# A mixture-of-experts layer on eight cores: a fourth w1 buffer, w2 loads in quarters, and the routing transposes moved

## What is computed

```python
x = _layernorm(x + attention(x))      # local window of 256 keys plus 64 pooled latents, 16 heads, gated
x = _layernorm(x + ffn(x))

# ffn: 8 experts of 1024 -> 4096 -> 1024, two chosen for each token
router_logits = x @ router_w.T + router_b + 0.1 * expert_weights
router_probs = softmax(router_logits)
top_p, top_i = jax.lax.top_k(router_probs, 2)
top_p = top_p / top_p.sum(axis=-1, keepdims=True)
h = gelu(jnp.einsum('bsd,edh->bseh', x, w1) + b1)
expert_out = jnp.einsum('bseh,ehd->bsed', h, w2) + b2
return (top_p[..., None] * jnp.take_along_axis(expert_out, top_i[..., None], axis=2)).sum(axis=2)
```

## Time and profile before

| | us |
|---|---|
| median of 2 runs | 5319.88 (5317.14 to 5322.62) |
| the profiled execution | 5318.32 |
| its span on the slowest core, core 2 | 5316.8 |
| spans of the 8 cores | 5295.5 to 5316.8 |
| PE busy | 4527.2 (85%) |
| DVE busy | 973.5 (18%) |
| ACT busy | 902.9 (17%) |
| POOL busy | 326.1 (6%) |
| DMA | 346.66 MB, mean 65 GB/s |

### The profile page before, as it was taken

The page is one execution under the profiler, slowest core; times in us unless marked ns, Lnnn a source line. Parts: engine busy times, 40 slices in busy tenths (PEclk is TensorE's granted clock), DMA queues, the critical chain, the costliest instruction groups (busy, mean ns, idle before and its releaser), DMA issues.

```text
span 5316.8 us, 72833 instructions; the slowest of 8 cores (5295.5 to 5316.8 us)
## 1 busy us (share of the span) xinstructions
PE 4527.2 (85%) x29399; PEld 2996.8 (56%) x29608; DVE 973.5 (18%) x3181; ACT 902.9 (17%) x1493; POOL 326.1 (6%) x622
## 2 busy tenths in 40 slices
PE   8865565555469999999999999999999999999993
PEld 8533333333227475665747566584756758476671
DVE  1344555544401010000101000010100001010004
ACT  0011111111120302112030211203021120302112
POOL 1000000000000101000010100101010010100000
PEclk5866665566589999999999999999999999999996
DMA  6120000000163433444343443434344343444431
GB/s 156 43 53 20 20 21 11 21 21 21 49 144 68 78 72 62 84 71 76 68 79 70 67 81 70 78 66 80 74 70 78 66 82 62 80 79 65 82 56 64
DMA packets 121848, 346.66 MB, mean 65 GB/s; under 512 B 32874, under 2 KB 33002, under 8 KB 112370
## 3 DMA queue, kind: packets, MB, share of 16 engines
q0 software_dynamic: 86768, 281.11, 30.5%
q1 hardware_dynamic: 34754, 60.87, 3.5%
HBM read 601.97 MB, written 20.97 MB: 117 GB/s over the span
## 4 chain that ended last, share of the span: by engine, by line
PE 79%; DVE 9%; DMA 4%; issue 4%; ACT 1%; another core or an unknown queue 1%; DVEq 1%; ACTq 0%; SPq 0%; POOL 0%; POOLq 0%
PE pb L1049 34%; PE pb L1023 32%; DMA w1b<-w 3%; PE pb L577 2%; PE pb L256 2%; PE pb L750 2%; PE pb L477 1%; DVE Pt L654 1%; PE pb L844 1%; PE pb L316 1%; DVE comb L589 1%; PE pb L634 1%; PE pb L736 1%; DMA x_in<-x_comb 1%
## 5 line engine op out<-in xcount | busy, mean ns | idle before, releaser
L1023 PE MATMUL pb<-x1T_sb,w1b 128*128 128x512 bf16 x8016 | 1793.4, 384 | 167.2 <-DMA w1b<-w 85.0
L1049 PE MATMUL pb<-w2b,hT 128*128 128x256 bf16 x16384 | 1791.1, 273 | 16.9 <-ACT hT L1031 16.9
L1049 PEld LDWEIGHTS pb<-w2b,hT 128*128 128x128 bf16 x16384 | 1602.0, 98 | 209.5 <-issue 24.3
L1023 PEld LDWEIGHTS pb<-x1T_sb,w1b 128*128 128x128 bf16 x8192 | 807.6, 99 | 1149.6 <-issue 210.4
L1031 ACT ACTIVATE hT<-pb,b1all 128x512 bf16<-128x512 f32 x1024 | 703.2, 687 | 2876.8 <-PE pb L1023 2874.7
L1059 DVE SCALAR_TENSOR_TENSOR acc<-pb,c_sb,acc 128x256 f32<-128x256 f32 x512 | 247.7, 484 | 3521.1 <-PE pb L1049 3521.1
L94 POOL DMA_DIRECT2D w1b<-w x512 | 270.2, 528 | 2859.8 <-PE pb L1023 1655.6
L647 ACT ACTIVATE Pt<-pb 128x384 bf16<-128x384 f32 x256 | 122.0, 490 | 445.3 <-PE pb L634 441.6
L677 PE MATMUL pb<-Vroll,Pt 128*128 128x65 bf16 x768 | 84.1, 235 | 79.7 <-DVE Pt L654 43.5
L634 PE MATMUL pb<-QT,Kroll 128*128 128x128 bf16 x768 | 117.6, 298 | 31.3 <-PE pb L677 9.8
L94 POOL DMA_DIRECT2D w2b<-w x64 | 33.8, 528 | 1740.3 <-PE pb L1049 1620.1
(11 more groups left out here) (132 smaller groups left out, 1458.2 us busy)
## 6 DMA issues: line engine op xcount, KB each, us to landing
w1b<-w POOLq DMA_DIRECT2D x512, 256.0 KB, 3.7
w2b<-w POOLq DMA_DIRECT2D x64, 2048.0 KB, 13.7
x_in<-x_comb SPq DMA_DIRECT2D x34, 512.0 KB, 3.5
x_tc<-x_comb SPq DMA_DIRECT2D x16, 512.0 KB, 4.0
x1s<-x_tc SPq DMA_DIRECT2D x16, 512.0 KB, 2.6
acc<-x1s SPq DMA_DIRECT2D x1, 8192.0 KB, 73.5
out<-acc SPq DMA_DIRECT2D x16, 512.0 KB, 2.6
x1Ts<-x1T_tc SPq DMA_DIRECT2D x16, 256.0 KB, 2.7
```

The costliest lines, as they stand in the source:

```text
L1023: e.matmul(PB[bk][:, :], w1b[sl][:, kc * 128:(kc + 1) * 128], x1T_sb[:, kc * 2048 + Tt * 1024 + nh * 512: kc * 2048 + Tt * 1024 + (nh + 1) ...
L1049: e.matmul(PB[ob][:, 0:256], hT[:, f * 1024 + tcl * 128: f * 1024 + tcl * 128 + 128], w2b[sl2][:, f * 256:(f + 1) * 256], start=(f == 0), ...
```

## The change

It has four parts.

- **w1 buffers.** Four instead of three; at the start of stage 3 four blocks are loaded, and each block's end triggers the load of the block four further on. Room for the buffer (2 KB on each partition) comes in part from `id_b`, which goes together with its load, and from a narrower `stat`.
- **w2 loads.** Each load of a quarter is issued as four DMAs of a fourth of its columns (128 x 2048), one behind the other; only the first waits. The consumer waits for all four.
- **Routing transposes.** The transpose (L906) and the copy (L910) go from the end of each chunk. In their place, 16 transposes in four rounds, with one copy of 8 x 512 for each round, stand between stage 2 and the first matmul of stage 3, in PSUM banks 6 and 7. Each round waits for the copy of the round before it.
- **The gate.** `FGATE` now ends with `CC` of the last chunk in place of its `CTEV`.

```diff
-        id_b = sb("id_b", [128, 128], BF16)
-        stat = sb("stat", [128, 64], F32)
+        stat = sb("stat", [128, 48], F32)
-        p.new_sem("gs_idb")
-        IDB = p.dma("g", id_b[:, :], ident_in, "gs_idb")
+        IDB = None
...
-                    p.op("t", lambda e, tc=tc:
-                         e.transpose(PB[5][0:8, 288:416], c_sb[:, tc * 8:(tc + 1) * 8], id_f[:, :]),
-                         deps=[CC, rtr_rd[1 - rslot]])
-                    CTMM = p.mark("t")
-                    CTEV = p.op("v", lambda e, tc=tc:
-                                e.tensor_copy(cT[0:8, tc * 128:(tc + 1) * 128], PB[5][0:8, 288:416]),
-                                deps=[CTMM], mark=True)
-                    rtr_rd[rslot] = CTEV
+                    cc_toks.append(CC)
+                    rtr_rd[rslot] = CC
...
-                w1b = [sbf1(f"w1b{i}", [128, 1024], BF16) for i in range(3)]
+                w1b = [sbf1(f"w1b{i}", [128, 1024], BF16) for i in range(4)]
...
-                    sl = idx % 3
+                    sl = idx % 4
                     tok = p.dma("g", w1b[sl][:, :], w1_in[e_, f, :, :], f"w1sem{sl}",
-                                deps=[w1_war[sl]] + (FGATE if idx < 3 else []))
+                                deps=[w1_war[sl]] + (FGATE if idx < 4 else []))
...
-                    tok = p.dma("g", w2b[sl][:, :], w2_in[e_, dq, :, :], f"w2sem{sl}",
-                                deps=[w2_war[sl]] + (FGATE if idx < 2 else []))
+                    tok = None
+                    for c4 in range(4):
+                        tok = p.dma("g", w2b[sl][:, c4 * 2048:(c4 + 1) * 2048],
+                                    w2_in[e_, dq, :, c4 * 2048:(c4 + 1) * 2048], f"w2sem{sl}",
+                                    deps=([w2_war[sl]] if c4 == 0 else []) +
+                                         (FGATE if idx < 2 and c4 == 0 else []))
...
+                load_w1(3)
                 load_w2(0)
                 load_w2(1)
+
+                ct_ev = None
+                for rnd in range(4):
+                    cb = 6 + rnd % 2
+                    for j in range(4):
+                        tcg = rnd * 4 + j
+                        p.op("t", lambda e, tcg=tcg, j=j, cb=cb:
+                             e.transpose(PB[cb][0:8, j * 128:(j + 1) * 128],
+                                         c_sb[:, tcg * 8:(tcg + 1) * 8], id_f[:, :]),
+                             deps=[cc_toks[tcg], EPB[6] if cb == 6 else EPB[7], ct_ev])
+                    tkc = p.mark("t")
+                    ct_ev = p.op("v", lambda e, rnd=rnd, cb=cb:
+                                 e.tensor_copy(cT[0:8, rnd * 512:(rnd + 1) * 512],
+                                               PB[cb][0:8, 0:512]),
+                                 deps=[tkc], mark=True)
+                CT_LAST = ct_ev
...
-                            if iw1 + 3 < len(seq_w1):
-                                load_w1(iw1 + 3)
+                            if iw1 + 4 < len(seq_w1):
+                                load_w1(iw1 + 4)
```

More of the change, by code:

```diff
@@ L434, in build_program @@
                 CC = None
+                cc_toks = []
                 LEXP = None
@@ L945, in build_program @@
                 CCLAST = CC
-                CT_LAST = rtr_rd[1]
                 EPB5X = pb5_ex
@@ L973, in build_program @@
                             b1_in.rearrange("e p f -> p e f"), "b1sem", deps=FGATE)
-                for i in range(3):
+                for i in range(4):
                     p.new_sem(f"w1sem{i}")
@@ L977, in build_program @@
                     p.new_sem(f"w2sem{i}")
-                w1_war = [None, None, None]
+                w1_war = [None, None, None, None]
                 w2_war = [None, None]
```

## The result

Part of the executions, of both kernels and of some in the experiments, ran with the clock of one die held lower, for which my range of 5200 to 5256 us had no room (with them the medians are 5455.79 us for the changed kernel, 12 runs, and 5815.41 us for the one before, 10 runs), so all times compared below, also those of the experiments, are of the others. These took 5225.01 to 5253.70 us with the change and 5316.03 to 5322.62 us before; their ratio is 0.984, with a 95% interval of 0.9809 to 0.9871. The profiled execution of the changed kernel took 5230.22 us, against 5318.32 before: 88.1 us less. My 5220 lies 10 us under it. What follows is about the 88 us.

The account below looks back on a forecast made before the run. PE bounds the kernel in the expert lines, standing at each phase handover for a w1 block queued behind w2. 5318.3 - 61 (buffer) - 25 (clock) + 0 (quarters) - 14.4 (transposes) + 1.3 (stage 3 start) gave 5220 us, range 5200 to 5256.

Parts of the forecast that it names:

- The fourth buffer: Phase handovers of the experts: one more w1 block in place shortens PE's waits for w1, 61 us less.
- its landing stays: Phase handovers: the fifth w1 block, still behind w2, lands when the fourth did, so each wait shrinks by 3.45 us.
- the expected hit of POOL's late issue: Experts: POOL's late w2 issue meets one handover instead of four; such waits were 6.42 to 6.52 us, not about 3.8.
- The clock: Experts: with shorter waits PE's matmuls mostly keep the full clock; 25 us less, 6 of 31 us staying.
- The assumption between the rows: Phase handovers: waits of 2.5 us and less keep the full clock; the trace has none between 1.04 and 3.76.
- The quarters: POOL's queue: w2 loads in four pieces move the same bytes one behind the other, so 0 us change.
- The transposes: Stage 2: without the transpose DVE starts the next chunk sooner, 0.9 us for each of 16 chunks, 14.4 us less.
- 0, if another wait was as late: Stage 2: low end of the saving from moving the routing transposes, no gain if another wait ends as late.
- The start of stage 3: Start of stage 3: `x1T_sb` lands some 15 us earlier, but the wait for ACT grows by as much; +1.3 us.
- the low clock: Rival, experts: waits near 2 us still lower the clock and some hits stay, 5250 us; chance 0.14.
- the pieces in series: Rival, POOL's queue: each added w2 piece pays 2.4 us ahead of the w1 blocks, 5363 us; chance 0.04.
- the full gain: Rival, phase handovers: all waits go as quarters land sooner in the early phases too, 5197 us; chance 0.16.

Follow-up runs that it names:

- e2: The kernel before with the fourth w1 buffer alone (w2 loads whole, transposes in their old place): 5233.11 us.
- e6: The changed kernel with each phase's last w2 load issued in four pieces behind the w1 loads of blocks 2, 4, 6 and 8 of the next phase: 5203.68 us.
- e4: The changed kernel with the small load of `b1all` ahead of `x1T_sb` and `acc` on SP's queue: 5221.6 us.
- e3: The kernel before with the w2 loads in quarters alone, three w1 buffers: 5311.89 us.
- e1: The kernel before with the routing transposes moved behind stage 2 and the new gate alone: 5324.7 us, beside 5320.1 before.
- e8: The changed kernel with two added DVE operations that nothing needs after `c_sb` of each chunk: 5229.86 us.
- e9: The changed kernel without the eight multiplications by the latent mask, which leaves the causal mask of the latent attention out: 5216.85 us.
- e5: The changed kernel with six added DVE operations that nothing needs after `c_sb` of each chunk: 5266.81 us.

## Why the prediction was right or wrong

**The fourth buffer, -61 us: right.** The w1 waits of the slowest core fell by 65.8, and the mean of the cores agrees (88.7 us off phases 2 to 16, with the clock). That core 7's first waits (5.24, 2.91, 1.50, 2.31) come near the 5.0, 3.4, 2.5, 2.3 that I worked out for core 2 is luck: core 2 itself now waits 0.33, 0.31, 1.28 and 0.36 us there, and core 7 had 3.85, 3.74, 3.98 and 3.70 before. The long early waits fall on one core of a pair, and not on the same one each time; my list put them down to core 2. The list of waits also adds up to nearly 23 us with its hit, where I wrote 21. One step inside it failed: "its landing stays". In phase 15 of core 2 it did (14.03 us after, 14.06 before), but on core 7 the block lands 15.45 us into phase 16 (4912.22 less 4896.77), where 14.3 was usual on that core. e2, whose w2 loads are whole, has it too (15.2 us in phases 7, 8 and 10), so the pieces are not why. It may be the other core's traffic; that was not tried. PE stood 0.8 to 1.5 us there in six of the phases 6 to 16, and the expected hit of POOL's late issue did not come on core 7, which made up for it.

**The clock, -25 us: right within 5 us.** The experts shrank by 85.8, of which 65.8 are waits, so 20 us of the 31 at half clock came back. e6 gives the floor, 3357 us without a wait: core 7 lies 29 us over it, of which 19.2 are w1 waits, so 10 us or a little less are left where I had left 6. The assumption between the rows was half right: 2.44 us (e2) kept the full clock, 2.31 us (phase 5 after) lowered it, 1.50 did not. A stretch after the wait of 1.50 us (phase 4) and one after that of 2.31 (the columns as in the windows above):

```profile
2211.50:2216.00 4.50, 4.43 (x21) 2.08 (x22) 0.00 (x0) 1.37 (x2) 0.28 (x1) 1.00 0.75 139
...
2438.00:2444.00 6.00, 6.00 (x21) 2.38 (x20) 0.00 (x0) 1.38 (x2) 0.32 (x1) 0.72 0.36 68
```

So it is not the length of the wait alone that decides: 2.31 us lowered the clock and 2.44 did not. In e4 a wait of 2.43 us on core 4 lowered it too, with 98.54 us for the same 448 matmuls that take 96.85 at the full clock:

```profile
2190.21 98.54 PE L1036 MATMUL pb<-x1T_sb,w1b 128*128 128x512 bf16 x448 [2.43 <-DMA w1b<-w]
```

**The quarters, 0: right in size**, at +0.1 us from issue to landing in phase 15 of e3, and a gain by the way that I had put under the buffer: 48 DMAs a phase move POOL's late issue off the handover.

**The transposes, -14 us: wrong, and this is the step that failed.** "The chain of DVE sets the end", I wrote, so that 0.9 us go for each chunk. They went, at the place that I named. But further down the chain stand 16 matmuls that run at either clock, and I priced them as fixed, though the profile's row of granted clock (0.5 to 0.6 through this stage) said that they are not. Two of 14 us remained on the mean of the cores (1068.7 to 1066.8), and 0.9 at the gate, which now follows the last `c_sb` by 0.5 us in place of 1.4; e1 shows it in isolation and e8 in reverse. I had named "0, if another wait was as late" as an end of this term, but looked for a wait and not for a clock. The profile's row before, 40 slices of 133 us in tenths of full speed, of which stage 2 takes the fifth to the eleventh:

```profile
PEclk5866665566589999999999999999999999999996
```

**The start of stage 3, +1.3 us: right**, at +2.4. `x1T_sb` lands 27.6 us after the gate, 19 sooner than before (I said some 15), and it bought nothing, for the reason given. The quarters alone (e3) bring it to 26 to 29 us over the cores. The rows that answer to the earlier trace rows:

```profile
1465.23 9.20 PE L1036 MATMUL pb<-x1T_sb,w1b 128*128 128x512 bf16 x32 [22.28 <-DMA x1T_sb<-x1Ts]
1517.64 2.72 PE L1036 MATMUL pb<-x1T_sb,w1b 128*128 128x512 bf16 x6 [43.21 <-ACT hT L1044]
...
1515.52 1.28 ACT L1044 ACT_TABLE_LOAD   x1 [80.94 <-DMA b1all<-b]
```

e4 shows it from the other side: with the biases first, phase 2 starts 22 us sooner.

**The sum.** 5220 against 5230: -86 came as -85.8, in which waits of 5 us more and clock of 5 us less cancelled, and the miss is stage 2. Of the rivals, neither the low clock nor the pieces in series nor the full gain came about.

## What to carry to other kernels

A load that is triggered by the end of one phase and stands in one queue ahead of the next phase's small loads costs its transfer, less what the buffers cover, at every handover. Another buffer hides a block's worth of it; splitting the load does nothing by itself, but lets the pieces be issued between the small loads (e6), which removes the wait. Before a saving on a dependent chain is counted, look for matmuls on the chain at a granted clock between 0.5 and 1: they can hand the time back, and here the savings came in steps (2.0 us, then 16.6), so several sizes should be tried. And when one transfer will land sooner, read what stands last in the same queue: here 128 KB of biases behind 12 MB held everything.

## What the runs showed of the hardware

- The time of a stage whose matmuls begin at half clock does not follow its dependent chain: with -0.9, -1.7 and +2.55 us a chunk (changed, e9, and e5, the first two against the kernel before, the last against the changed one) the stage moved by -2, -18.6 and +33 us. The same 16 matmuls took 5.1 to 6.8 us in the single chunks of e5 and e9. How long the clock stays low depends on when the matmuls come, not only on how long PE was idle before (2.43 us lowered it in e4, 2.44 did not in e2); what sets the moment of its rise stays open.
- In POOL's queue DMAs follow each other without a gap that shows: in the changed kernel, in phase 15, 2.17 MB of quarters and w1 blocks moved at 197 GB/s, as whole loads did.

```profile
DMA packets 618, 2.17 MB, mean 197 GB/s; under 512 B 64, under 2 KB 64, under 8 KB 618
```

- Two queues took turns by packets (257 and 257 in the earlier trace rows). Quartering the packets of one (e3) let the other's 4 MB land 26 to 29 us after the gate over the cores, in place of 44 to 47, while `b1all`, the last of its queue, came no sooner (74.7 us after the gate on the mean, 74.1 before).
